# Reordering the openings of two stages: roots and a first layer ahead of tables and a second turn in the MLP, one block's weighing ahead of constant columns in the combination

## The reference, cut to what matters

```python
    # end of _L0_xattn_ref: gelu MLP, then a norm; x = x + result
    xt = xt + h
    return layernorm(xt, g_norm_out, b_norm_out)

    # _L0_ffn_ref, on the layernorm of x
    logits = jax.nn.relu(x @ rw1 + rb1) @ rw2 + rb2
    vals, ids = jax.lax.top_k(logits, K)
    probs = jax.nn.softmax(vals, axis=-1)
    ...
    y = eo[ids_f, pos_c] * (probs_f * keep)[:, None]
    return y.reshape(Bx, Tx, K, Cx).sum(axis=2)

    x = x + _L1_xattn_ref(_layernorm(x, axis=-1), ctx_768, ...)
```

## Time and profile before

| | |
|---|---|
| three runs | 932.19, 935.39, 935.05 us; median 935.05 us |
| span of the profiled execution | 935.4 us; no time outside the span is listed for it, and the run of 935.39 us agrees with it |
| PE busy | 710.3 us (76%) |
| DVE busy | 673.2 us (72%) |
| POOL busy | 564.8 us (60%) |
| ACT busy | 473.4 us (51%) |
| mean granted PE clock | 0.799 |

### The profile page before, as it was taken

One profiled execution on the slowest core, in us unless ns is written; L12 is line 12 of the kernel. 1 busy time (PEld: TensorE's weight loads), 2 busy tenths in 40 slices (PEclk: granted clock), 3 DMA queues, 4 the chain that ended last, 5 costly groups with the idle time before them and its releaser, 6 DMA issues. The chain is left out here.

```text
span 935.4 us, 20537 instructions
## 1 busy us (share of the span) xinstructions
PE 710.3 (76%) x6072; PEld 508.4 (54%) x6072; DVE 673.2 (72%) x3212; ACT 473.4 (51%) x1318; POOL 564.8 (60%) x931
## 2 busy tenths in 40 slices
PE   0686898979883999972498528998888874799970
PEld 0353554545483656631275426766666652699970
DVE  6898989978524688769111167598998887699974
ACT  3566576735200455450133175577777761577740
POOL 7688877766526544210677667345777767277770
PEclk9767787957555999996599855798988885899995
DMA  6300112997213977700365330000000002698928
GB/s 143 57 25 10 41 45 64 86 88 96 40 45 140 290 250 257 243 23 0 39 115 132 88 137 1 2 4 13 25 26 25 25 28 76 216 279 264 260 69 270
DMA packets 98829, 94.41 MB, mean 101 GB/s; under 512 B 37511, under 2 KB 82302, under 8 KB 98142
## 3 DMA queue, kind: packets, MB, share of 16 engines
q1 hardware_dynamic: 91268, 79.34, 33.1%
q0 software_dynamic: 6592, 13.58, 6.0%
q10 hardware_dynamic: 858, 0.17, 0.1%
HBM read 47.76 MB, written 43.19 MB: 97 GB/s over the span
## 5 line engine op out<-in xcount | busy, mean ns | idle before, releaser
L2402 POOL DMA_INDIRECT expert_pairs<-e_ys,e_home x78 | 75.4, 967 | 38.4 <-issue 23.5
L1742 POOL TENSOR_SCALAR a_kb<-a_kr,a_m,a_bk 128x128 f32<-128x128 f32 x128 | 57.9, 452 | 44.4 <-ACT a_kr L1981 32.3
L1760 POOL DMA_INDIRECT expert_slots<-r_rows,r_slotu x64 | 63.3, 989 | 30.3 <-DVE r_rows L2136 15.1
L950 DVE MATCH_REPLACE8 work<-m,work 128x64 f32<-128x64 f32 x384 | 75.7, 207 | 0.0
L1484 POOL DMA_INDIRECT ex_rows<-rows,slot_source x32 | 30.7, 960 | 52.7 <-POOLq L1163 43.2
L937 DVE MAX8 m<-work 128x8 f32<-128x64 f32 x384 | 57.0, 209 | 0.0
L825 PE MATMUL psf<-filmw,us 97*128 97x512 f32 x64 | 51.6, 902 | 3.0 <-ACT FO L846 2.9
L1815 PE MATMUL a_pss<-a_kb,a_qt 32*64 32x256 f32 x512 | 41.5, 463 | 13.9 <-ACT a_pp L1966 11.7
L2168 DVE TENSOR_REDUCE a_mx<-a_pss 128x8 f32<-128x512 f32 x64 | 43.9, 686 | 8.1 <-PE a_pss L1815 7.8
L2369 PE MATMUL e_ps<-e_XH,e_wh 128*128 128x256 f32 x156 | 48.1, 308 | 1.5 <-DVE e_XL L2414 1.5
L1536 ACT ACTIVATE ex_hs<-ex_psh,vec 128x512 f32<-128x512 f32 x32 | 22.0, 687 | 51.2 <-PE ex_psh L1517 50.5
(11 more groups left out here) (464 smaller groups left out, 2418.2 us busy)
## 6 DMA issues: line engine op xcount, KB each, us to landing
expert_slots<-rt_unfilled SPq DMA_DIRECT2D x151, 130.0 KB, 2.6
ahead<-folded_weights SPq DMA_DIRECT2D x20, 386.0 KB
e_wf<-folded_weights SPq DMA_DIRECT2D x19, 386.0 KB, 4.2
planes<-rt_zeros SPq DMA_DIRECT2D x4, 1024.0 KB
ew<-in_L_ffn_ew SPq DMA_DIRECT2D x16, 256.0 KB, 4.0
pair_y<-expert_pairs SPq DMA_DIRECT2D x16, 256.0 KB, 5.6
e_xr<-expert_slots SPq DMA_DIRECT2D x27, 130.0 KB, 3.3
folded_weights<-fold_done SPq DMA_DIRECT2D x8, 384.0 KB, 4.3
```

What stands on the lines that cost most here:

```text
L950: return own.did(dve.match_replace(wk_[x.j][:, h, :], m8[x.j][:, h, r, :], src[:, h, :], TAKEN))
L1742: m = pool.tensor_scalar(kb[a.j][:, :, h, :], k, m4[:, h:h + 1], bk4[:, h:h + 1], ALU.mult, ALU.add)
L1760: pool.indirect_dma_start(G.slots, bass.IndirectOffsetOnAxis(ap=slot[:, b, k, t:t + 1], axis=0), rb[b % NB][:, k, t, :], None).then_inc(se ...
L2402: pool.indirect_dma_start(G.pair, bass.IndirectOffsetOnAxis(ap=home[i % NY][:, k:k + 1], axis=0), ys[i % NY][:, k, :], None).then_inc(kept ...
```

## The change

It moves instructions and adds none but for branches. In the MLP stage POOL does the first root of block 0 first of all, then the zeros, the root of block 1, the unfilled tile, the biases of block 0, the root of block 2, the biases of block 1, the pick and iota tables, and the biases of block 2; from step 1 on the loop is the one of before. PE and ACT do the first layer of block 0 ahead of the turn of block 1. In the combination stage ACT weighs block 0 ahead of the three copies of extra columns, and DVE computes `cst` ahead of everything else.

```diff
             @block.gpsimd
             def _(pool):
+                def root_of(q, b):
+                    pool.wait_ge(var[q], b + 1)
+                    inverse_root(pool, step, st[q], root[q])
+
+                def add_biases(b):
+                    rows = slice(b * TB, (b + 1) * TB)
+                    pool.wait_ge(s["xs"], b + 1)
...
+                root_of(0, 0)
+                pool.memset(zeros[:], 0.0).then_inc(s["zeros"], 1)
+                root_of(0, 1)
+                step.did(pool.iota(unfilled_i[:], pattern=[[1, STILE // P]], base=SPARE, channel_multiplier=STILE // P))
...
+                add_biases(0)
+                root_of(0, 2)
+                add_biases(1)
                 step.then(pool.tensor_tensor(pick[:], G.ident[:, 0:32], G.ident[:, 32:64], ALU.add))
...
-                pool.memset(zeros[:], 0.0).then_inc(s["zeros"], 1)
...
-                for t in range(-2, NBLK + 1):
+                add_biases(2)
+                for t in range(1, NBLK + 1):
...
             def _(pe):
...
+                turn_first(0)
+                for t in range(NBLK + 3):
+                    if t == 0:
+                        hidden(0)
                     if blk(t + 1):
...
+                        turn_first(t + 1)
+                    if 0 < t < NBLK:
+                        hidden(t)
...
             def _(act):
...
+                keep_first(0)
+                for t in range(NBLK + 3):
+                    if t == 0:
+                        gelu(0)
                     if blk(t + 1):
...
+                        keep_first(t + 1)
+                    if 0 < t < NBLK:
+                        gelu(t)
...
                 for b in range(NBLK):
                     weigh_rows(b)
+                    if b == 0:
+                        keep_constants()
...
+                dve.wait_ge(cm["rows_of"], 1)
+                dve.tensor_tensor(cst[:, 0:D], G.att["bo"][:], psd[:, 0:D], ALU.add).then_inc(cm["cst"], 1)
                 dve.wait_ge(s["zero"], 1)
```

More of the change, by code:

```diff
@@ L1204, in _ @@
-                for t in range(-2, NBLK + 1):
+                add_biases(2)
+                for t in range(1, NBLK + 1):
                     for q, b in ((0, t + 2), (1, t - 1), (2, t - 1)):
                         if blk(b):
-                            pool.wait_ge(var[q], b + 1)
-                            inverse_root(pool, step, st[q], root[q])
+                            root_of(q, b)
                     if blk(t + 2):
[L1210 to L1213, removed]
+                        add_biases(t + 2)
@@ L1215, in _, with turn_first @@
             @block.tensor
             def _(pe):
-                for t in range(-1, NBLK + 3):
-                    if blk(t + 1):
[L1219 to L1230, removed]
+                def turn_first(b):
+                    pe.wait_ge(s["xs"], b + 1)
+                    after(pe, s["xf"], b)
+                    after(pe, s["xf1"], b - 3)
+                    for k in range(TB):
+                        mm = pe.transpose(pst[:, k * P:(k + 1) * P], xs[b % 2][:, k, :], G.ident[:])
+                    mm.then_inc(s["turned"], 1)
@@ new lines, in hidden @@
+                def hidden(b):
+                    pe.wait_ge(s["xf"], b + 1)
+                    for c in range(NH):
+                        after(pe, r_sb[c], b - 2)
+                        pe.matmul(psh[c][:], w1[:, c * P:(c + 1) * P], xf[b % 2][:], start=True, stop=True).then_inc(h_ps[c], 1)
+                turn_first(0)
+                for t in range(NBLK + 3):
+                    if t == 0:
+                        hidden(0)
+                    if blk(t + 1):
+                        turn_first(t + 1)
+                    if 0 < t < NBLK:
+                        hidden(t)
@@ L1289, in _, with keep_first, gelu @@
                 act.preload_act_table(ACT.Gelu)
-                for t in range(-1, NBLK + 3):
-                    if blk(t + 1):
[L1292 to L1298, removed]
+                def keep_first(b):
+                    act.wait_ge(s["turned"], b + 1)
+                    act.activation(xf[b % 2][:], pst[:], ACT.Identity, scale=G.vec[:, gv:gv + 1],
+                                   bias=G.vec[:, bv:bv + 1]).then_inc(s["xf"], 1)
+                def gelu(b):
+                    for c in range(NH):
+                        act.wait_ge(h_ps[c], b + 1)
+                        act.activation(hs[b % 2][:, c, :], psh[c][:], ACT.Gelu, bias=G.vec[:, b1 + c:b1 + c + 1]).then_inc(h_sb[c], 1)
+                keep_first(0)
+                for t in range(NBLK + 3):
+                    if t == 0:
+                        gelu(0)
+                    if blk(t + 1):
+                        keep_first(t + 1)
+                    if 0 < t < NBLK:
+                        gelu(t)
                     if blk(t - 3):
```

18 lines of the change are left out of this document (9 added, 9 removed).

## The result

| | before | changed |
|---|---|---|
| five runs each, median | 935.39 us (932.19 to 939.04) | 925.14 us (924.43 to 933.35) |
| ratio, 95% interval | | 0.9889, 0.9852 to 0.9926 |
| span of the profiled execution | 935.4 us | 932.0 us |
| mean granted PE clock in it | 0.799 | 0.802 |

The profiled execution of the changed kernel is the run of 933.35 us, the slowest of its five, so its span alone would tell a wrong story. Such a profile has to be read stage by stage, each from its own start. All ratios and all means of spans in this text leave out executions more than 1.5% above the fastest of their kernel.

The account below looks back on a forecast made before the run. DVE and POOL were taken to bound the MLP's opening up to XT, and late ACT weighing the combination. 0.95 - 0.65 + 4.2 = 4.5 us off 935.4 gave 930.9, forecast as 930.5 us; range 926.5 to 933.8.

Parts of the forecast that it names:

- The collisions: MLP opening: DVE's normalising is held beside POOL's memsets and bias additions, 3.02 instead of 1.11 us beside biases.
- The first rival: MLP opening: collisions cost nothing, the MLP gains 2.5 to 4.0 us, total gain 6.7 to 8.2 us; chance 18%.
- the second normalising: MLP opening, block 1: unfilled tile and two biases hold DVE, xs complete at 303.5 against 303.55 before, nothing gained.
- What is gained in this opening is what DVE and POOL gain: MLP opening: only DVE's and POOL's gain up to XT counts, since an early PE waits there; 0.95 us.
- The loss of 0.65 us behind PE's hole: MLP, PE idling before XT: its clock may fall; bounds 0 and 1.7 us, 0.65 taken as the even chance.
- the MLP's term: MLP stage: nb and XT of block 0 0.95 us earlier, less 0.65 us for PE's clock.
- The combination: Combination stage: block 1's weighing starts at 540.2 instead of 544.41, gaining 4.2 us; bounds 2.9 and 5.1.
- a late cst: Combination: were cst still late, ACT would keep its old start and the part be worth only three copies, 0.2 us.
- The attention's clock: Attention's opening: PE's clock may rise later, each further tile at half clock costing 2.6 us; a slower kernel, chance 8%.
- the attention's tiles change their length: Attention stage: a sign that the forecast is wrong, as only the start of these tiles was to move.

Follow-up runs that it names:

- PE's old order: Changed kernel with the order of before on PE and ACT (block 1's turn ahead of block 0's first layer): ratio 0.9948, nb at 23.7 us.
- the wait that was always met: Changed kernel plus a POOL wait before later blocks' biases that named the wrong block, so it held nothing: ratio 0.9869.
- MLP alone: Changed kernel with the combination's functions of before: ratio 0.9981, nb at 21.9 us, last logits at 125.6 us.
- the fourth group's two: Changed kernel with DVE's cst back at its old place, ratio 0.9932; changed kernel with ACT's extra columns ahead of the first weighing again, ratio 0.9866.

## Why the prediction was wrong

- **The collisions** were right in kind and nearly in size. The forecast had the first normalising at some 2.6 us beside the zeros, 2.38 measured, and the third at about 3, 3.07, in which each bias held one operation (1.29 and 1.31 us). The root came 2.5 us earlier counted from the statistics (1.37 us behind them; 3.88 before). The first rival, that collisions cost nothing, is refuted by the run that moved the zeros.
- **The step that failed** is the second normalising: "unfilled tile, then the two biases, take DVE's turns; xs of block 1 complete at 303.5". It was complete at 304.55, which is 302.1 on the clock of before, 1.4 us earlier. One line's instructions, 302.4 to 304.6:

```profile
L211 DVE TENSOR_SCALAR mlp_xs<-XT,mlp_ln_mv,mlp_ln_rstd x4: 343/382/1292, 302.5 to 303.3; 128x128 f32<-128x128 f32 x4
```

Its four operations took 343 ns at the shortest, 382 in the median and 1292 at the longest. So one of them was held: the fourth, begun at 303.26 behind the start of the first bias (303.11), ended 0.07 us after it. The first three had begun before that bias. The unfilled tile (302.43 to 303.14) ran beside them and held none of them for more than 0.08 us (0.42, 0.34 and 0.34 us), and the second bias came too late to hold any. All later steps inherit the 1.4 us: 0.95 + 1.4 = 2.35, 2.4 measured. The error was to let every POOL instruction of the stretch collide, whatever DVE had already begun or finished. (The Trainium skill, SBUF — State Buffer, Who interferes with whom, calls it an exclusive lock that whoever issues first has for the whole instruction. The held operation, which ended with the bias that it met, agrees with it.)
- **"What is gained in this opening is what DVE and POOL gain"** was wrong as a reading of before, though it did not spoil the number. DVE's wait of 3.04 us for PE at 312.97 stood in the timeline and was not read. Had only POOL's order been changed, DVE and POOL could have gained 2.4 us up to nb, and the wait for PE would have left 0.6. In the changed kernel POOL's queue decides, as the forecast had it: the root for nb begins 1.3 us behind its statistics. PE's product has that much to spare, which is why bringing it 2.9 us later (PE's old order) cost nb only 1.8.
- **The loss of 0.65 us behind PE's hole** was charged as an even chance, and that was about right. Six profiles have the changed kernel's MLP: its own two, the wait that was always met, MLP alone, and the fourth group's two. In three the hole was 1.41 to 1.83 us, the product behind it took 3.74 us at a granted clock of 1.00, and the last logits came at 124.4 to 124.5. In three it was 2.38 to 2.51 us, the clock fell to 0.50 behind it, the product took 5.36 to 5.37 us, and the last logits came at 125.5 to 125.6: 1.1 us of loss. The profile of the result happened to be of the first kind. On average of the six the MLP gives 2.2 us (125.0, against 127.2 on average of three profiles with the old MLP), where 0.3 were forecast. The second normalising's 1.4 us are most of that gap; the rest is what the profiles of before differ in (nb at 24.3 to 24.9).
- **The combination** was right: 4.2 forecast, 4.3 measured; first weighing 3.7 us behind the first product (3.6), 0.60 us of pause (1), the second weighing at 540.45. The forecast saw that a late cst would leave only the copies' 0.2 us. It took the new order of ScalarE for a part of the gain, and that is worth nothing beside the early cst. Without the early cst it is worth some 1.7, not 0.2: the forecast counted the copies' own length and not their wait for PE, 1.54 us at 541.89.
- **The attention's clock** was kept as a rival for a slower kernel, with "or if the attention's tiles change their length" as the mark of a wrong forecast. They did, to the other side: the rise came earlier in eight of eleven profiles, for 1.7 us on average, if the change has a part in it at all. "A stage that starts at another moment may find the rise a tile or more later" had no row for its direction; it should have stood with both signs, up to 3 us each, in the range. That a rise some 9 us earlier helped the measured time was luck as far as the forecast goes.

So some 2 of the 5.8 us of the miss are the MLP's term, and that part is shown. The rest is open: it lies partly in the granted clock of the executions, to which the attention's start belongs, and partly in what the change gives at equal clock beyond its two stages.

## What to carry to other kernels

Read every wait on the chain that you count along: DVE's 3.04 us for PE, left unread, decided 1.8 us. When two engines collide, go operation by operation, since a POOL instruction holds the one DVE instruction that meets it, not a whole group. And before a chain is sped up, ask which single instruction all its members wait for: here one sum of 0.29 us behind unrelated waits carried 4.3 us. Where untouched stages vary by 11 us between executions, compare stages from their own start, and runs at equal clock.

## What the runs showed of the hardware

- VectorE's additions and multiplications of two tiles in SBUF (128x512) took 1.80 and 1.64 us beside GpSimd's additions, and 0.69 us alone; GpSimd's took 1.72 instead of 1.27 beside them. Adding a product out of PSUM took 0.65 to 0.69 us, with biases running beside it too (at 311.81 in the changed kernel).
- Between executions of the same code but for a wait that was always met, PE's clock at the start of the attention rose some 9 us earlier or later (0.69 over the third window from a_mx, or 0.73 over the second), and the first four tiles took 26.2 or 23.2 us by it.
- Pauses of PE of 2.38, 2.46 and 2.51 us were followed by a stretch at 1.2 GHz (0.50), in which a product of 3.74 us took 5.36 to 5.37; behind pauses of 1.41 to 2.10 us, in six profiles, it took 3.74.
